# Score and row matmuls of a fused attention and feed-forward kernel, split into four 32-column strips each

## The reference

```python
q, k, v = (bitnet_linear(xn, w, s) for w, s in ...)   # sign of the weights, scaled per output
# 32 query heads of 16 dims; 8 key and value heads, each shared by 4 query heads
scores = q @ k.T / sqrt(16)                            # 32 heads x 1024 x 1024
attn = softmax(scores)
out = bitnet_linear(attn @ v, wo, so)
hidden = silu(xn @ gate_w.T) * (xn @ up_w.T)           # 1792 wide
return x + out + hidden @ down_w.T
```

## Time and profile before

| what | value |
|---|---|
| median of 3 runs | 504.78 us (504.18 to 508.95) |
| span of the profiled execution | 502.6 us |
| busy: PE, DVE, ACT, POOL | 95%, 83%, 70%, 19% |
| PE in the chain that ended last | 86% |
| granted TensorE clock, mean | 1.000 |

### The profile page before, as it was taken

The page is one execution under the profiler, slowest core; times in us unless marked ns, Lnnn a source line. Parts: engine busy times, 40 slices in busy tenths (PEclk is TensorE's granted clock), DMA queues, the critical chain, the costliest instruction groups (busy, mean ns, idle before and its releaser), DMA issues.

```text
span 502.6 us, 10338 instructions
## 1 busy us (share of the span) xinstructions
PE 479.6 (95%) x4186; PEld 163.0 (32%) x4186; DVE 417.2 (83%) x487; ACT 350.3 (70%) x655; POOL 94.4 (19%) x138
## 2 busy tenths in 40 slices
PE   0899999999999999999999999999999999999996
PEld 0564444434332222222222222222222233333442
DVE  6879868676778999999999999999999955223986
ACT  1853643343229999999999999999999978874000
POOL 4212334534323000000000000000000113241021
PEclk9999999999999999999999999999999999999999
DMA  8862782641103802102102211111120034452321
GB/s 260 252 123 81 159 171 38 187 91 22 23 0 42 148 23 63 40 24 65 39 25 63 40 37 49 41 53 32 41 62 24 14 96 107 110 148 79 105 82 45
DMA packets 31302, 39.02 MB, mean 78 GB/s; under 512 B 6608, under 2 KB 20816, under 8 KB 31256
## 3 DMA queue, kind: packets, MB, share of 16 engines
q1 hardware_dynamic: 22232, 27.34, 19.0%
q0 software_dynamic: 8304, 10.95, 11.8%
q10 hardware_dynamic: 720, 0.08, 0.1%
HBM read 33.24 MB, written 10.35 MB: 87 GB/s over the span
## 4 chain that ended last, share of the span: by engine, by line
PE 86%; ACT 8%; DVE 3%; issue 1%; DMA 1%; SPq 0%; ACTq 0%; DVEq 0%
PE ps L1301 25%; PE ps L1131 19%; PE ps L1235 12%; PE ps L1140 8%; ACT room L705 6%; PE ps L1207 5%; PE ps L1194 5%; PE ps L1110 3%; PE ps L1335 3%; PE ps L1271 2%; ACT osb L716 1%; DMA hlo<-x 1%; DVE nmx L838 1%; PE ps L1048 1%; PE ps L1102 1%
## 5 line engine op out<-in xcount | busy, mean ns | idle before, releaser
L838 DVE TENSOR_REDUCE nmx<-ps 128x1 f32<-128x1024 f32 x248 | 284.6, 1216 | 14.5 <-PE ps L1140 14.2
L705 ACT ACTIVATE room<-ps 128x512 f32<-128x512 f32 x512 | 272.4, 598 | 20.9 <-PE ps L1271 11.0
L1301 PE MATMUL ps<-room,vcur 128*32 128x256 f32 (+1 forms) x1880 | 159.1, 410 | 4.3 <-ACT osb L716 4.1
L1140 PE MATMUL ps<-kA,qst 48*128 48x512 f16 x496 | 140.4, 382 | 0.0
L1235 PE MATMUL ps<-qst,kB 50*128 50x512 f16 x432 | 132.2, 382 | 0.8 <-DVE room L937 0.5
L1131 PE MATMUL ps<-room,wf 128*128 128x512 f16 x448 | 100.6, 379 | 0.0
L1301 PEld LDWEIGHTS ps<-room,vcur 128*32 128x32 f32 x1880 | 37.1, 108 | 100.8 <-issue 55.6
L686 ACT ACTIVATE room<-ps,gsc 128x512 f32<-128x512 f32 x28 | 19.2, 687 | 61.6 <-PE ps L1131 61.6
L1131 PEld LDWEIGHTS ps<-room,wf 128*128 128x128 f16 x448 | 42.4, 98 | 55.1 <-issue 7.2
L1235 PEld LDWEIGHTS ps<-qst,kB 50*128 50x128 f16 x432 | 26.8, 93 | 89.1 <-ACT room L705 79.8
L543 POOL TENSOR_TENSOR hlo<-room,hhi 128x512 f16<-128x512 f32 x28 | 34.1, 1217 | 87.4 <-ACT hhi L616 87.4
(11 more groups left out here) (136 smaller groups left out, 320.1 us busy)
## 6 DMA issues: line engine op xcount, KB each, us to landing
qst<-q_scratch SPq DMA_DIRECT2D x32, 192.0 KB, 3.6
o_scratch<-osb SPq DMA_DIRECT2D x16, 256.0 KB, 2.3
q_scratch<-parts SPq DMA_DIRECT2D x12, 256.0 KB
hlo<-x SPq DMA_DIRECT2D x8, 256.0 KB, 6.1
parts<-x POOLq DMA_DIRECT2D x8, 256.0 KB, 3.5
wf<-gate POOLq DMA_DIRECT2D x14, 128.0 KB, 3.9
wf<-up POOLq DMA_DIRECT2D x14, 128.0 KB, 6.0
wd<-down POOLq DMA_DIRECT2D x1, 1792.0 KB, 14.3
```

Source lines behind the costliest of these rows:

```text
L705: nc.scalar.activation(probs[:, s % 2, r, :], ps[:, bank_of(gp, s, i), :], ACT.Exp, scale=gam_reg[par][r]).then_inc(scores_free, 1)
L838: nc.vector.tensor_reduce(nmx[:, hf, idx:idx + 1], bank_pair(idx % 2), AX.X, ALU.max, negate=True).then_inc(rows_free, 1)
L1140: return nc.tensor.matmul(ps[:, 2 * (idx % 2) + b, :], qst[low:low + KROWS, par, hf, head, qt * P:(qt + 1) * P], kA[low:low + KROWS, par, ...
L1301: mm = nc.tensor.matmul(ps[32 * r:32 * r + 32, 7, of], vcur[:, par, key_tile(r, j), :], probs[:, s % 2, r, of], start=(j == 0 and part == ...
```

## The change

In `scores`, the loop of the first 108 steps, each score tile (128 output partitions) becomes four matmuls of 32 weight columns, each writing 32 partitions of the same bank; the semaphore counts on the last. Each row half does the same in a new function, `strip_rows`. The moving operand of each strip is the whole one of before, 512 columns. The tile of the array is 64 rows x 32 columns instead of 64 x 128. The first key head's rows (between the feed-forward products), the late steps, the value matmuls and the transposes stay.

```diff
+            def strip_rows(par, hf, idx, b):
+
+                head, qt = idx // (HALF // P), idx % (HALF // P)
+                low = b * HI
+                for c in range(0, P, 32):
+                    mm = nc.tensor.matmul(ps[c:c + 32, 2 * (idx % 2) + b, :],
+                                          qst[low:low + KROWS, par, hf, head, qt * P + c:qt * P + c + 32],
+                                          kA[low:low + KROWS, par, :], start=True, stop=True)
+                return mm
...
-                    nc.tensor.matmul(ps[:, score_bank(e), :],
-                                     kB[low:low + SROWS, par, kt % (TT // 2) * P:(kt % (TT // 2) + 1) * P],
-                                     qst[low:low + SROWS, par, hf, r, :], start=True, stop=True).then_inc(scores_ready, 1)
+                    for c in range(kt % (TT // 2) * P, (kt % (TT // 2) + 1) * P, 32):
+                        mm = nc.tensor.matmul(ps[c % P:c % P + 32, score_bank(e), :],
+                                              kB[low:low + SROWS, par, c:c + 32],
+                                              qst[low:low + SROWS, par, hf, r, :], start=True, stop=True)
+                    mm.then_inc(scores_ready, 1)
...
-                        mm = half_rows(1 - par, hf, idx, 1 - half)
+                        mm = strip_rows(1 - par, hf, idx, 1 - half)
...
-                            half_rows(1 - par, hf, idx, half).then_inc(rows_ready, 1)
+                            strip_rows(1 - par, hf, idx, half).then_inc(rows_ready, 1)
```

## The result

The changed kernel takes 508.65 us (median of 20 runs, 507.12 to 511.77) against 504.87 us before (20 runs): +3.8 us, ratio 1.0077, 95% interval 1.0062 to 1.0092. Its profiled execution has a span of 505.9 us at a granted clock of 1.00. I had forecast 514 us: the sign was right, the size was two and a half times too large.

The account below looks back on a forecast made before the run. TensorE was taken to set the pace, VectorE nearly full behind it. 190 half-steps x (0.044 starts + 0.006 loads) = 9.5 us: profiled 502.6 to 512.1, median 2.2 above, so 514 us; range 504 to 526.

Parts of the forecast that it names:

- What bounds the kernel: In the loop: TensorE sets the pace at 1.11 us a half-step; VectorE, at 1.13, has 0.25 us slack a block.
- The spread of the starts: Score and row strips: eight starts 0.007 us apart, paid once, add 0.044 us a half-step.
- the low bound: Strip starts: if strips on different row halves start as close as the pair, only 0.020 us a half-step is added.
- The other figure: Strip starts by the Trainium skill's about 4 ns per further tile: 0.025 us a half-step, sum some 4 us smaller.
- Exposed loads: First weight loads of strips after a change-over, not hidden by streaming: 0.006 us added a half-step.
- The change-over: Between score/row tiles and values, twice a half-step: hangs on tile rows, so both stay 0.31 us, no gain.
- Counted from the last start: The 0.31 us change-over runs from the last strip's start, so the spread of starts lengthens the half-step.
- The rival of a change-over for each column strip: Each strip waits only for its own columns; staggers cancel: 0 to 2 us, 505 to 507; shared chance 0.22.
- Covered half-steps: At a block's start two half-steps lie under ACT's chain with 0.4 us room, leaving 14 of 16, 190 in all.
- Issue, instruction fetch, eight strips at once: Loop's added matmuls and loads: no cost taken; serial strips (598) or issue limit (650) together had chance 0.08.
- stagger at its low bound: Case of smallest start spread, or change-over per strip: 505 to 509.8 us, chance 0.22.
- Within 1%: Whole kernel counted as same, 499.7 to 509.8 us: chance 0.25, against slower 0.73 and faster 0.02.

Follow-up runs that it names:

- experiment 4: Kernel before and changed kernel, each with VectorE's row maxima over 512 of 1024 columns and exponentials' scale cut: ratios 1.0014 and 1.0076 to the kernel before.
- Experiment 9: Kernel before with the late down-projection strips moved ahead of the value matmuls in each late step: 504.3 us, one execution.
- experiment 2: Changed kernel with only score tiles in strips, row halves back to 64 x 128: 623.6 us at clock 1.00, 884 us at mean clock 0.64.
- experiment 3: Changed kernel with row halves as two strips of 64 x 64, score strips still 64 x 32: 893.4 and 893.6 us, ratio 1.77, clock 0.64.
- experiment 5: Changed kernel, values over 64 of 128 keys, maxima halved, exponentials' scale cut: 485.9 and 487.2 us at clock 1.00, 637 and 634 at 0.70.
- experiment 6: Kernel before (full score tiles and row halves), values over 64 of 128 keys, maxima halved, scale cut: 506.5 us at clock 1.00, 688 to 691 at 0.69.
- experiment 7: Changed kernel, values over 64 of 128 keys, whole maxima, exponentials' scale cut: 507.3 us at clock 0.99, 635 to 637 at 0.70.

## Why the prediction was off, point by point

**What bounds the kernel: right.** TensorE alone is in the chain in the body of a block of both kernels, and experiment 4 took 40% of VectorE's work away for nothing. That VectorE would stand idle for some 10 us did not come: it was 4.5. The 10 rested on a half-step of 1.16, and at 1.127 TensorE is still just ahead of VectorE's 1.13.

**The spread of the starts: the term that was mis-sized, and the cause of the miss.** I took 0.044 a half-step from the late strips' 0.007 a start and gave 0.020 as the low bound. It measured 0.021. The earlier trace rows were the nearest rows in shape, f16 with 512 columns, but not in history: they come behind f32 strips in the same tiles and inherit their distance. Experiment 9 shows that on the very line I had read. The low bound was the right number by luck. I had reasoned that columns cost 0.007 and the step to the other half of the rows 0.003; in fact each of the seven steps between eight f16 strips costs 0.003. The other figure that I gave and didn't use, 0.025 a half-step, was nearer than my 0.044, which I preferred because no row had eight tiles. Over 190 half-steps it is 4.4 of the 5.7 us by which the forecast was above the measurement, 9.5 against 3.8.

**Exposed loads: 0.006 forecast, nothing measured** (1.1 us). A 32-column load shows the same 9 ns as the full tile's, and eight of them are exposed no more than one: there is nothing of the 0.2 us that I had priced for loads one after another. Strips of 64 show that the term is real for another width.

**The change-over: kept at 0.31, as forecast, for a wrong reason.** I concluded that rows alone make it, from one pair of rows. The earlier trace rows is the exception, not the rule: the transpose of 16 columns follows full 128 x 128 tiles freely. The trace of before held the counter-example in every block, the same transpose behind the value strips:

```profile
267.89 0.64 PE L1301 MATMUL ps<-room,vcur 128*32 128x256 f32 x8
268.46 0.28 PE L1151 MATMUL ps<-ident,nmx 128*16 128x128 f32 x1
```

The last value strip starts at 268.15, the transpose at 268.46: 0.31 between two kinds of full height. It looks as if a 16-column matmul alone runs in the mode of the full tile; that is an inference from these two distances. The Trainium skill's sentence that a change of tiling mode drains TensorE (TensorEngine Tiling (Array Packing), Tiling Modes), which I had set against the earlier trace rows, fits experiments 2, 3, 5 and 6. For this change both readings gave two change-overs, so it cost nothing in the sum. It wasn't exactly neutral: 0.309 instead of 0.312 after the values, 0.6 us given back.

**Counted from the last start: right.** 0.308 from the last score start to the first value start, whether full tiles or strips of 64 or 32 stand before it. The rival of a change-over for each column strip falls with it: it would have made that distance shorter by the spread.

**Covered half-steps: one, not two.** At a block's start I let two half-steps go free under ScalarE's chain. From value to value only one distance of a block is covered, 1.508 us against 1.502 before. The other fifteen all grow, fourteen by 0.018 and the one with the transpose by 0.023, so a block gave 0.28 and not 14 x 0.018 = 0.25. This error of 0.4 us in all went the other way: with the 4.4 of the starts, the 1.1 of the loads and the 0.6 after the values it makes up the 5.7 us of the miss.

**Issue, instruction fetch, eight strips at once: right, no cost shows.** 24 matmuls and 24 loads go through in 1.127 us; the fetch queue grew from 0.54 to 0.87 MB and from 0.5% to 0.7%.

**The chances.** 508.65 us is inside the range, and inside the case "stagger at its low bound", which I gave 0.22, half of what I gave the wrong value. Within 1% had 0.25, slower by over 1% 0.73; it was 0.77%.

No experiment with the whole work was faster than the kernel before; experiment 5 was, with half of the values' rows and half of the maxima left out. With whole maxima VectorE needs 18.1 us of a block's 18.37, so a loop without change-overs could gain 3.4 us at most; that is an estimate, and experiment 7 leaves it open.

## What to carry to other kernels

Splitting a tile into column strips that all go together cost TensorE the sum of their starts here, 0.003 us each, once before a change-over, and bought nothing, since each strip streams the whole moving operand. Neighbours should have the same tile in rows and in columns: with one kind in strips and the other not, kinds that had started together stood 0.32 apart, and the kernel took 24% longer at the full clock. Before a distance is taken from a row, look at what ran in the same tiles before it: here a group of strips kept the spacing of the group before it.

## What the runs showed of the hardware that was not expected

In some executions of experiments 2, 3, 5, 6 and 7 the mean granted clock was only 0.64 to 0.70. In those of them that have a trace, of 3, 6 and 7, it fell at 156 to 157 us, a few us after the loop began. Slices of the span in experiment 6, then in experiment 3:

```profile
PEclk9999999995555555555555555555555555899999
```

```profile
PEclk9999999555555555555555555555555555569999
```

With full clock up to the loop, it is at half, 1.2 instead of 2.4 GHz, for nearly all of the loop, and full again in the late steps. PE counts as busy 100% of that stretch, here 200 to 500 us of experiment 6:

```profile
200.00:500.00 300.00, 300.00 (x1821) 50.08 (x1821) 103.89 (x151) 170.92 (x320) 9.44 (x23) 0.50 0.09 24
```

It came in four of six executions of experiment 2, both of 3, two of four of 5, and three of four of 6 and 7; in none of 20 runs of the changed kernel did it. TensorE's busy time at the full clock doesn't set them apart: in the loop of experiment 5 it was 208 of 220 us, in that of the changed kernel 243 of 248. In each of these kernels either the values use fewer rows of the array, or score and row tiles run one after another instead of side by side; whether that is the reason wasn't tried. The cut scale of the exponentials is not: experiment 4 has it too, and its 14 executions kept 0.99 to 1.00.
